# A selective scan with a routed feed-forward net on one core: GpSimd's products two states at a time, ranking inside its PSUM bank, new engine orders

## The chip, the cores and the metric

The kernel runs on one core of one Trainium2 chip. The metric is the device time of one execution in microseconds (us); smaller is better. Three runs of the kernel before took 1288.14, 1292.01 and 1292.46 us, a median of 1292.01. The engines are PE (TensorE), DVE (VectorE), ACT (ScalarE), POOL (GpSimd) and SP (SyncE, which here only issues transfers).

## The reference, cut to what matters

The input x is 16 sequences of 512 steps and 128 channels. Each goes through two layers with residual sums.

```python
# layer 1: selective scan, D_INNER = 256, D_STATE = 16
xn = layernorm(x)
x_proj, z = split(xn @ W_in + b_in)
u = silu(x_proj)
B, C = split(u @ W_xproj + b_xproj)
dt = softplus(u @ W_dt + b_dt)
#   per step t: h = h * exp(dt * A) + (dt * u) * B ;  y = sum over states of h * C + D * u
x = x + (y * silu(z)) @ W_out + b_out
# layer 2: shared expert and 8 routed experts, the best 2 weighed
xt = layernorm(x)
scores = softmax(xt @ gate_w.T)
chosen = top_k(scores + gate_bias, 2)
x = x + sum over e of mlp_e(xt) * weight_e + mlp_shared(xt)
#   mlp(x) = (silu(x @ w1.T) * (x @ w3.T)) @ w2.T, inner width 256
```

## The kernel before, in words

**Tiling.** Channels lie on the 128 partitions and the 512 steps of a sequence along the free axis. 256 inner channels are 2 halves, so one sequence has 2 x 16 = 32 scans, numbered 0 to 31 ("states" below), each over 128x512.

**One state's way.** ACT writes the decay exp(dt*A) into one of two PSUM banks (`da`, task `decay`, L589). POOL writes (dt*u)*B into one of four SBUF slots (`dbu`, L673). DVE scans the two (`scan`, L773). The product with C is then made either by DVE (`mul`, L781: the scan went to its PSUM bank, the product goes to a slot of `hc`) or by POOL (`hcp`, L681: the scan went to the `hc` slot, which is multiplied in place). `BY_DVE` says which: the 15 even states up to 28; POOL has the other 17. PE adds each product to `y_acc` by four transposing matmuls (`red`, L920). `hc` has four slots, so that scan or product of state a waits for the reduction of state a-4; `decay` of state a waits until state a-2 has left its bank.

**The second layer.** 9 experts x 2 halves = 18 units a sequence. PE makes `h1` and `h3` of a unit, each from three matmuls over 512 columns (L938), in three PSUM banks that take turns; ACT makes `silu` (L625), DVE `g` = silu * h3 (L815), PE `eo` (L907, 16 matmul records an expert), ACT scales by the router's weight (`sc`, L632) and DVE adds (`comb`, L823). Two more banks ("mixed") are shared in turn by all other matmuls: transposes of x and y (`x_t`, `gy`, `split`), `xp`, `z`, `bc`, `dl`, `proj`, `route`, `eo`.

**Router.** After `route`, ACT takes the exponential in the route bank and DVE does eight small steps (`rank.0` to `rank.7`, L697 to L717). Scores and biased scores lie in SBUF; the table of comparisons lies in the route bank. Step 4 (L708) subtracts the biased scores from themselves, 128x256 out of two SBUF operands. Step 7 (L717) writes `comb`, the weights.

**Normalisation.** DVE makes means and variances (L743, L751) and adds EPS (L754); POOL raises to the power -0.5 (L646, L649); DVE makes the shift (L761).

**Order.** Every engine follows a list written by hand or by a planner outside the kernel: `ORDER` is one pass of a loop ("window"), `START_ORDER` and `END_ORDER` are straight code before and after. `scan.5+1` is state 5 of the sequence after the window's own. Work of four sequences overlaps in a window. SP's queue loads x and the residual, and spreads B and C over all partitions in four groups a sequence (`spread`), each waiting until the states that read the old rows are done. Engines meet only at semaphores.

## Time and profile before

| what | us |
|---|---|
| median of three runs | 1292.01 |
| the profiled execution, whole | 1290.66 |
| its span, first to last instruction | 1288.5 |

The span and its rows come from the profiled execution; 2.2 us of that execution lie outside the span. A row of the engines gives busy time, not use: an engine that waits at a semaphore isn't busy. Rows that group instructions give the mean duration of one; neighbours on an engine overlap a little, so that the distance between two starts is shorter than the duration. "DMA" is the share of the core's transfer engines.

### The profile page before, as it was taken

Reading aid. Unit: us, or ns where it says so; the run is one execution under the profiler, and the core shown is the slowest. Engines: PE = TensorE matmul, PEld = TensorE weight load, DVE = VectorE, ACT = ScalarE, POOL = GpSimd, SP = SyncE. Lnnn points to the kernel's source line nnn. Section 1 sums busy time; section 2 is a strip of 40 time slices with the busy share of each in tenths; the row PEclk is TensorE's granted clock in tenths of the full one; section 3 lists DMA queues with packets and bytes.
Section 4 is the critical chain, followed back from the end, with each engine's and each line's share of the span. In section 5 each row is a group of like instructions: output and inputs, shape, how many; then the busy total and the mean of one; then the engine's idle time right before and its main releaser. Section 6 shows DMA issues by size and latency. Waiting matters only on the chain.

```text
span 1288.5 us, 25674 instructions
## 1 busy us (share of the span) xinstructions
PE 1179.8 (92%) x7200; PEld 946.2 (73%) x7200; DVE 1174.2 (91%) x1833; ACT 1126.6 (87%) x1965; POOL 1112.8 (86%) x902
## 2 busy tenths in 40 slices
PE   4565899999999999999999999999999999999998
PEld 2334587877878787787778777777878778788887
DVE  1779899999999999999999999999999999999954
ACT  6674889999998999999899999989989998999854
POOL 2999899898999989899998989999898999998700
PEclk8776899999999999999999999999999999999999
DMA  8233331605234160523415052331505243250000
GB/s 305 121 146 125 133 148 39 250 1 207 82 132 155 54 232 0 205 81 137 150 62 225 0 205 81 144 142 67 220 0 210 77 152 135 71 208 9 10 9 9
DMA packets 47942, 152.74 MB, mean 119 GB/s; under 512 B 4512, under 2 KB 29472, under 8 KB 31392
## 3 DMA queue, kind: packets, MB, share of 16 engines
q1 hardware_dynamic: 47904, 152.28, 31.3%
q8 instruction: 18, 0.29, 0.1%
q14 instruction: 20, 0.16, 0.0%
HBM read 147.03 MB, written 5.24 MB: 118 GB/s over the span
## 4 chain that ended last, share of the span: by engine, by line
POOL 27%; issue 23%; PE 22%; DVE 19%; ACT 7%; DVEq 1%; DMA 0%; POOLq 0%; ACTq 0%; SPq 0%
POOL dbu L673 16%; PE h L938 10%; POOL hc L681 7%; DVE da L773 6%; PE mixed L907 5%; DVE hc L773 5%; PE y_acc L920 4%; POOL dt_s L661 3%; DVE g L815 2%; ACT L625 2%; ACT silu L625 2%; ACT da L589 1%; DVE acc L823 1%; DVE stats L743 1%; DVE hc L781 1%
## 5 line engine op out<-in xcount | busy, mean ns | idle before, releaser
L673 POOL TENSOR_TENSOR dbu<-w_s,b_all 128x512 f32<-128x512 f32 x512 | 650.3, 1289 | 5.7 <-DVE da L773 3.0
L681 POOL TENSOR_TENSOR hc<-hc,c_all 128x512 f32<-128x512 f32 x272 | 350.5, 1292 | 82.1 <-DVE hc L773 80.6
L589 ACT ACTIVATE da<-dt_s,a_neg 128x512 f32<-128x512 f32 x512 | 346.7, 692 | 84.2 <-DVE hc L781 70.0
L773 DVE TENSOR_TENSOR_SCAN hc<-da,dbu 128x512 f32<-128x512 f32 x272 | 328.1, 1211 | 12.0 <-PE y_acc L920 10.9
L920 PE MATMUL y_acc<-ident,hc 128*128 128x128 f32 x2048 | 295.0, 280 | 32.5 <-POOL hc L681 27.3
L773 DVE TENSOR_TENSOR_SCAN da<-da,dbu 128x512 f32<-128x512 f32 x240 | 292.6, 1219 | 27.4 <-ACT da L589 15.1
L920 PEld LDWEIGHTS y_acc<-ident,hc 128*128 128x128 f32 x2048 | 247.5, 144 | 81.5 <-POOL hc L681 36.2
L907 PE MATMUL mixed<-w_s,g 128*128 128x128 f32 x2304 | 283.4, 276 | 3.2 <-DVE g L815 1.2
L907 PEld LDWEIGHTS mixed<-w_s,g 128*128 128x128 f32 x2304 | 270.6, 192 | 15.4 <-DVE g L815 10.1
L938 PE MATMUL h<-x_hi,w_hi 128*128 128x512 f32 x576 | 264.1, 458 | 7.4 <-DVE g L815 2.9
L938 PE MATMUL h<-x_hi,w_lo 128*128 128x512 f32 x576 | 228.4, 396 | 0.0
L938 PE MATMUL h<-x_lo,w_hi 128*128 128x512 f32 x576 | 227.9, 396 | 0.0
L815 DVE TENSOR_TENSOR g<-silu,h 128x512 f32<-128x512 f32 x288 | 193.4, 676 | 24.0 <-PE h L938 9.8
L625 ACT ACTIVATE silu<-h 128x512 f32<-128x512 f32 x288 | 158.6, 600 | 30.6 <-PE h L938 29.0
L781 DVE TENSOR_TENSOR hc<-da,c_all 128x512 f32<-128x512 f32 x240 | 163.9, 683 | 8.2 <-DVE da L773 2.6
L632 ACT ACTIVATE mixed<-mixed,comb 128x128 f32<-128x128 f32 x512 | 141.1, 337 | 20.4 <-PE mixed L907 20.3
L938 PEld LDWEIGHTS h<-x_hi,w_hi 128*128 128x128 f32 x576 | 109.3, 190 | 60.5 <-DVE g L815 32.5
L938 PEld LDWEIGHTS h<-x_hi,w_lo 128*128 128x128 f32 x576 | 108.4, 188 | 25.7
L589 ACT ACT_TABLE_LOAD x94 | 120.6, 1283 | 2.5 <-DVE hc L781 0.8
L938 PEld LDWEIGHTS h<-x_lo,w_hi 128*128 128x128 f32 x576 | 110.2, 191 | 12.1 <-issue 3.1
L625 ACT ACT_TABLE_LOAD x90 | 115.5, 1283 | 1.6
L823 DVE TENSOR_TENSOR acc<-mixed,acc 128x512 f32<-128x512 f32 x128 | 86.1, 673 | 8.7 <-ACT mixed L632 8.6
(77 smaller groups left out, 1063.6 us busy)
## 6 DMA issues: line engine op xcount, KB each, us to landing
b_all<-bc_rows SPq DMA_DIRECT2D x64, 1024.0 KB, 4.7
c_all<-bc_rows SPq DMA_DIRECT2D x64, 1024.0 KB, 6.8
xt<-in_x SPq DMA_DIRECT2D x16, 256.0 KB, 6.5
res<-in_x SPq DMA_DIRECT2D x16, 256.0 KB, 6.9
out<-acc SPq DMA_DIRECT2D x16, 256.0 KB, 2.3
silu<-in_w SPq DMA_DIRECT2D x6, 256.0 KB, 4.1
w_s<-in_w SPq DMA_DIRECT2D x1, 1152.0 KB, 6.9
bc_rows<-bc_rows_s SPq DMA_DIRECT2D x16, 64.0 KB, 1.6
```

Of the source, the lines that this page charges most:

```text
L589: act.activation(da[a % DA_SLOTS][:, :], dt_s[:, c, :], ACT.Exp, scale=a_neg[:, a:a + 1]).then_inc(decay_made, 1)
L625: act.activation(silu[:, a % SILU_SLOTS, :], h_tile("h1", a, n, off)[:, :], ACT.Silu).then_inc(silu_made, 1)
L632: last = act.activation(block_, block_, ACT.Copy, scale=comb[:, b, a - 1:a])
L673: pool.tensor_tensor(dbu[:, a % DBU_SLOTS, :], w_s[:, c, :], b_all[:, s, :], ALU.mult).then_inc(dbu_made, 1)
L681: pool.tensor_tensor(slot, slot, c_all[:, s, :], ALU.mult).then_inc(c_by_pool, 1)
L773: dve.tensor_tensor_scan(dst, ring[:, :], dbu[:, a % DBU_SLOTS, :], 0.0, ALU.mult, ALU.add).then_inc(scanned, 1)
L781: dve.tensor_tensor(hc[:, a % HC_SLOTS, :], da[a % DA_SLOTS][:, :], c_all[:, s, :], ALU.mult).then_inc(c_by_dve, 1)
L815: dve.tensor_tensor(g[:, a % G_SLOTS, :], silu[:, a % SILU_SLOTS, :], h_tile("h3", a, n, off)[:, :], ALU.mult).then_inc(g_made, 1)
L823: dve.tensor_tensor(acc[:, :, :], as_blocks(tile), acc[:, :, :], ALU.add).then_inc(freed, 1)
L907: last = pe.matmul(as_blocks(tile)[:, b, :], g[:, slot, b * P:(b + 1) * P], w2_s[:, at:at + DM], start=(f == 0), stop=(f == NF - 1))
L920: last = pe.matmul(y_acc[:, b, :], hc[:, a % HC_SLOTS, b * P:(b + 1) * P], ident[:, :], is_transpose=True, start=False, stop=(a % NS == NS ...
L938: last = pe.matmul(dst[:, :], w13_at(w, e, which, f), xx[:, :], start=(i == 0), stop=(i == len(parts) - 1))
```

## The change

1. **POOL works on pairs.** `dbu.k` now makes states 2k and 2k+1 in one instruction (128x1024, the operand dt*u repeated by a stride of zero), and `hcp.a` multiplies the slots of states a and a+1 by two rows of C. `dbu` has 8 slots in place of 4. The first scan of a pair waits for both products of `dbu`, and `hcp` waits for both scans.
2. **DVE has 16 states** in place of 15: 0, 1, 4, 5, ... 28, 29. POOL has 2, 3, 6, 7, ... 30, 31, eight pairs.
3. **Ranking reads its bank.** Scores and a second copy of the biased scores are kept in the route bank, so that no ranking step reads two SBUF operands. Step 3 becomes two instructions. The bank is now freed by step 7, not by step 6.
4. **EPS is added on POOL**, in `rs1` and `rs2` ahead of the power, with waits of its own.
5. **All orders are new.** The loop now runs over windows 4 to 13, and more of the program is straight code: START covers the first three sequences' scans.

Counted over one pass of the loop: ACT's table loads go from 13 to 14, POOL's instructions on 512 columns from 49 (32 + 17) to 24 on 1024 columns, DVE's products with C from 15 to 16. The other instructions of the loop are as many as before. In the whole program ACT's table loads go from 210 to 225.

```diff
-DA_SLOTS, DBU_SLOTS, HC_SLOTS = 2, 4, 4
+DA_SLOTS, DBU_SLOTS, HC_SLOTS = 2, 8, 4
+AT_ONCE = 2
+DBUS = STEPS // AT_ONCE
-BY_DVE = [0, 2, 4, 6, 8, 10, 12, 14, 16, 18, 20, 22, 24, 26, 28]
+BY_DVE = [0, 1, 4, 5, 8, 9, 12, 13, 16, 17, 20, 21, 24, 25, 28, 29]
 BY_POOL = [a for a in range(STEPS) if a not in BY_DVE]
+POOL_PAIRS = BY_POOL[::2]
...
 "pool":
-        hcp.7 dbu.10 dbu.11 rs1.0+1 dbu.12 dbu.13 hcp.9 hcp.11 dbu.14 dbu.15 hcp.13 dbu.16 rs2.0-1 dbu.17
+        dbu.15 rs1.0+2 hcp.26 dbu.0+1 hcp.30 dbu.1+1 dbu.2+1 dbu.3+1 hcp.2+1 resb.0 dbu.4+1 dbu.5+1 hcp.6+1
...
-                    act.wait_ge(route_steps, RANK_STEPS * (m + 1))
+                    act.wait_ge(*taken("route", 0, n, off))
...
                 elif what == "rs2":
+                    wait_apart(pool, moments2_made, m + 1)
+                    pool.tensor_scalar(var_eps2[:, :], moments2[:, :, 1], EPS, None, ALU.add).then_inc(var2_made, 1)
                     pool.wait_ge(var2_made, m + 1)
...
                 elif what == "dbu":
-                    c, s = a // NS, a % NS
+                    step = AT_ONCE * a
+                    c, s = step // NS, step % NS
...
-                    wait(pool, scanned, STEPS * m + a + 1 - DBU_SLOTS)
-                    pool.tensor_tensor(dbu[:, a % DBU_SLOTS, :], w_s[:, c, :], b_all[:, s, :],
-                                       ALU.mult).then_inc(dbu_made, 1)
+                    user, back = before(step + AT_ONCE - 1, DBU_SLOTS, STEPS)
+                    if not (isinstance(m, int) and m == 0 and back):
+                        pool.wait_ge(scanned, STEPS * (m - back) + user + 1)
+                    at = step % DBU_SLOTS
+                    pool.tensor_tensor(dbu[:, at:at + AT_ONCE, :], w_s[:, c, None, :].broadcast_to([P, AT_ONCE, T]),
+                                       b_all[:, s:s + AT_ONCE, :], ALU.mult).then_inc(dbu_made, 1)
                 elif what == "hcp":
                     s = a % NS
-                    pool.wait_ge(scanned, STEPS * m + a + 1)
+                    pool.wait_ge(scanned, STEPS * m + a + 2)
...
-                    slot = hc[:, a % HC_SLOTS, :]
-                    pool.tensor_tensor(slot, slot, c_all[:, s, :], ALU.mult).then_inc(c_by_pool, 1)
+                    at = a % HC_SLOTS
+                    pair = hc[:, at:at + 2, :]
+                    pool.tensor_tensor(pair, pair, c_all[:, s:s + 2, :], ALU.mult).then_inc(c_by_pool, 1)
...
                 elif i == 3:
-                    step = dve.tensor_tensor(biased[:, :, :], score[:, :, :],
-                                             gb_s[:, None, :].broadcast_to([P, NB, E]), ALU.add)
+                    for dst in (biased[:, :, :], other):
+                        step = dve.tensor_tensor(dst, score, gb_s[:, None, :].broadcast_to([P, NB, E]), ALU.add)
                 elif i == 4:
-                    step = dve.tensor_tensor(ahead, other, own, ALU.subtract)
+                    step = dve.tensor_tensor(ahead, other[:, :, None, :].broadcast_to([P, NB, E, E]), own, ALU.subtract)
...
                 elif i == 7:
-                    dve.wait_ge(*ranked)
                     wait(dve, scaled, E * m)
...
                 elif what in ("agg1", "agg2"):
-                    dve.wait_ge(done, m + 1)
-                    dve.tensor_scalar(var[:, :], mom[:, :, 1], EPS, None, ALU.add).then_inc(ready, 1)
...
                 elif what == "scan":
-                    dve.wait_ge(dbu_made, STEPS * m + a + 1)
+                    dve.wait_ge(dbu_made, DBUS * m + a // AT_ONCE + 1)
```

How the orders move work is seen at three places. On POOL, at the head of the loop, the kernel before has:

```order
L681 TENSOR_TENSOR hc<-hc,c_all 128x512
...
L673 TENSOR_TENSOR dbu<-w_s,b_all 128x512 x2
...
L646 TENSOR_TENSOR rstd<-var_eps,minus_half 128x4
...
L673 TENSOR_TENSOR dbu<-w_s,b_all 128x512
...
L681 TENSOR_TENSOR hc<-hc,c_all 128x512
```

and the changed one:

```order
L767 TENSOR_TENSOR dbu<-w_s,b_all 128x1024
...
L731 TENSOR_SCALAR var_eps<-moments 128x4
L733 TENSOR_TENSOR rstd<-var_eps,minus_half 128x4
...
L777 TENSOR_TENSOR hc<-hc,c_all 128x1024
...
L767 TENSOR_TENSOR dbu<-w_s,b_all 128x1024
...
L777 TENSOR_TENSOR hc<-hc,c_all 128x1024
```

The same products now come in instructions of twice the width, and the addition of EPS stands ahead of the power.

On DVE, the ranking steps 2 to 7 in the loop stand in the kernel before like this (`scan` is the SCALAR_TENSOR_TENSOR of L773, `mul` is L781):

```order
L703 TENSOR_TENSOR score<-mixed,inverse 128x32 [waits route_steps]
...
L705 TENSOR_TENSOR biased<-score,gb_s 128x32 [waits route_steps]
...
L708 TENSOR_TENSOR mixed<-biased 128x256 [waits route_steps]
...
L773 SCALAR_TENSOR_TENSOR da<-da,dbu 128x512 [waits dbu_made,decay_made]
...
L711 TENSOR_TENSOR mixed<-mixed,below 128x256 [waits route_steps]
...
L713 TENSOR_REDUCE rank<-mixed 128x32 [waits route_steps]
...
L717 SCALAR_TENSOR_TENSOR comb<-rank,score 128x32 [waits scaled]
```

and in the changed one (`scan` is L869, `mul` L877):

```order
L801 TENSOR_TENSOR mixed<-mixed,inverse 128x32 [waits route_steps]
...
L805 TENSOR_TENSOR biased<-mixed,gb_s 128x32 [waits route_steps]
L805 TENSOR_TENSOR mixed<-mixed,gb_s 128x32
...
L807 TENSOR_TENSOR mixed<-mixed,biased 128x256 [waits route_steps]
...
L869 SCALAR_TENSOR_TENSOR da<-da,dbu 128x512 [waits dbu_made,decay_made]
...
L810 TENSOR_TENSOR mixed<-mixed,below 128x256 [waits route_steps]
...
L812 TENSOR_REDUCE rank<-mixed 128x32 [waits route_steps]
...
L815 SCALAR_TENSOR_TENSOR comb<-rank,mixed 128x32 [waits scaled]
```

One operand of each step now lies in the bank ("mixed"), and one small instruction more is there.

On PE, in the loop, the transposes of y (`gy`) are the next user of the bank that `route` had. Before, `gy` follows ten tasks after `route`, the last of them (`eo`, a reduction, a unit's `h1`) being these:

```order
L907 MATMUL mixed<-w_s,g 128x128 [waits mixed_freed1,g_made]
L907 MATMUL mixed<-w_s,g 128x128 x7
...
L920 MATMUL y_acc<-ident,hc 128x128 [waits c_by_pool]
...
L938 MATMUL h<-x_hi,w_hi 128x512 [waits g_made]
...
L845 MATMUL mixed<-ident,y_s 128x128 [waits mixed_freed0]
```

In the changed order, from the same `eo` on (rows of like kind left out):

```order
L1003 MATMUL mixed<-w_s,g 128x128 [waits mixed_freed0]
...
L1034 MATMUL h<-x_hi,w_hi 128x512 [waits g_made]
...
L1016 MATMUL y_acc<-ident,hc 128x128 [waits c_by_pool]
...
L1034 MATMUL h<-x_hi,w_hi 128x512 [waits silu_made]
...
L1012 MATMUL y_acc<-ident,skip 128x128 [waits y_copied]
...
L941 MATMUL mixed<-ident,y_s 128x128 [waits mixed_freed1,y_copied]
```

Now 23 tasks stand between `route` and `gy`, eleven of them after that `eo`, so that the ranking has more of PE's work beside it.

## Rows read from the trace of the kernel before

**Rows 1.** The page: busy time, share of the span and instructions, by engine

```profile
PE 1179.8 (92%) x7200; PEld 946.2 (73%) x7200; DVE 1174.2 (91%) x1833; ACT 1126.6 (87%) x1965; POOL 1112.8 (86%) x902
```

**Rows 2.** Stretches: length, busy PE, PEld, DVE, ACT, POOL; clock, DMA share, GB/s

```profile
32.60:103.00 70.40, 38.03 (x162) 25.25 (x162) 56.83 (x57) 45.49 (x67) 69.72 (x55) 0.74 0.37 154
492.00:1090.50 598.50, 575.48 (x3584) 461.88 (x3584) 581.34 (x913) 557.31 (x977) 554.75 (x449) 1.00 0.33 124
1225.00:1288.50 63.50, 57.81 (x364) 50.47 (x361) 29.72 (x61) 31.12 (x77) 1.02 (x1) 0.99 0.03 9
```

**Rows 3.** DVE's timeline (start, length): the residual sum, once a window, eight windows apart

```profile
492.02 0.68 DVE L788 TENSOR_TENSOR res<-mixed,res 128x512 f32<-128x512 f32 x1
...
1090.57 0.68 DVE L788 TENSOR_TENSOR res<-mixed,res 128x512 f32<-128x512 f32 x1
```

**Rows 4.** Groups of instructions, 492.0 to 1090.5 us (count | busy, mean ns | idle before)

```profile
L673 POOL TENSOR_TENSOR dbu<-w_s,b_all 128x512 f32<-128x512 f32 x256 | 324.7, 1287 | 0.0
L681 POOL TENSOR_TENSOR hc<-hc,c_all 128x512 f32<-128x512 f32 x137 | 176.0, 1287 | 42.9 <-DVE hc L773 42.1
L589 ACT ACT_TABLE_LOAD x48 | 61.6, 1283 | 0.8
L881 PE MATMUL mixed<-xnT,win_s 128*128 128x512 f32 x64 | 31.5, 615 | 9.6 <-DVE acc L823 9.6
L661 POOL TENSOR_TENSOR dt_s<-soft,lin 128x512 f32<-128x512 f32 x16 | 22.0, 1378 | 0.0
L708 DVE TENSOR_TENSOR mixed<-biased 128x256 f32<-128x256 f32 x8 | 11.5, 1442 | 0.3
L845 PE MATMUL mixed<-ident,y_s 128*128 128x128 f32 x64 | 10.0, 279 | 8.4 <-DVE rank L713 8.4
L754 DVE TENSOR_SCALAR var_eps<-moments 128x4 f32<-128x4 f32 x16 | 9.9, 618 | 0.6
L649 POOL TENSOR_TENSOR rstd<-var_eps,minus_half 128x4 f32<-128x4 f32 x8 | 8.1, 1009 | 0.0
L717 DVE SCALAR_TENSOR_TENSOR comb<-rank,score 128x32 f32<-128x32 f32 x8 | 2.9, 364 | 0.0
L705 DVE TENSOR_TENSOR biased<-score,gb_s 128x32 f32<-128x32 f32 x8 | 2.4, 301 | 0.0
L703 DVE TENSOR_TENSOR score<-mixed,inverse 128x32 f32<-128x32 f32 x8 | 1.4, 180 | 0.0
```

**Rows 5.** Line 708 alone: shortest, median and longest of its instructions in ns

```profile
L708 DVE TENSOR_TENSOR mixed<-biased x16: 405/1440/1445, 163.3 to 1252.6; 128x256 f32<-128x256 f32 x16
```

**Rows 6.** POOL's timeline: a tiny fill, and products in a row

```profile
0.87 0.10 POOL L640 MEMSET minus_half<- 128x4 f32 x1
...
75.74 7.48 POOL L673 TENSOR_TENSOR dbu<-w_s,b_all 128x512 f32<-128x512 f32 x6
83.17 2.50 POOL L681 TENSOR_TENSOR hc<-hc,c_all 128x512 f32<-128x512 f32 x2
```

**Rows 7.** DVE's timeline: a scan, `g` and a product with C in a row

```profile
571.28 1.20 DVE L773 TENSOR_TENSOR_SCAN da<-da,dbu 128x512 f32<-128x512 f32 x1
572.40 0.67 DVE L815 TENSOR_TENSOR g<-silu,h 128x512 f32<-128x512 f32 x1
572.99 0.67 DVE L781 TENSOR_TENSOR hc<-da,c_all 128x512 f32<-128x512 f32 x1
```

**Rows 8.** The page's transfers: one group of C's rows, KB and us to landing

```profile
c_all<-bc_rows SPq DMA_DIRECT2D x64, 1024.0 KB, 6.8
```

**Rows 9.** Beginning, DVE's timeline: a two-operand split of weights

```profile
97.73 1.75 DVE L734 TENSOR_TENSOR w_lo<-silu,w_hi 128x512 fp32r<-128x512 f32 x1
```

**Rows 10.** The chain that ended last, near the end: seven units' matmuls, one `eo`

```profile
1249.53 4.92 PE h L938 x21
1254.44 1.78 PE mixed L907 x16
```

**Rows 11.** PE's timeline: one reduction

```profile
565.29 0.60 PE L920 MATMUL y_acc<-ident,hc 128*128 128x128 f32 x4
```

295 lines of the change are left out of this document (188 added, 107 removed).

## The prediction, made before the changed kernel ran

> **What bounds the kernel now.** I read the busy rows of the page first: PE 92%, DVE 91%, ACT 87%, POOL 86% [rows 1]. No engine stands out, so the stretches come next. In the middle the program is periodic: DVE's once-a-window sum starts at 492.02 and, eight windows later, at 1090.57 us [rows 3], which is 598.55 / 8 = 74.82 us a window. Divided by eight, the busy times of that stretch [rows 2] are DVE 72.7, PE 71.9, ACT 69.7 and POOL 69.3 us a window. The reader is to see two things. DVE is at 97%, and its load is the first floor; and all four are so close that taking work from one only uncovers the next. Each engine follows a fixed order, so what is left over (2.2 us above DVE's load) is the price of four orders that must mesh.
>
> The beginning is different. From 32.6 to 103.0 us POOL is busy 69.7 of 70.4 us, DVE 56.8 and ACT 45.5 [rows 2]: the second layer hasn't begun, and the products on POOL set the pace. At the end POOL is done, and PE works off the last units, busy 57.8 of 63.5 us [rows 2].
>
> The groups in the middle show the waits that bear on the change [rows 4]: POOL's `hcp` waited 42.1 us for scans, 5.3 a window; PE's `gy` waited 8.4 us (1.05 a window) for ranking, PE's matmuls of `xp` and `z` 9.6 us (1.2 a window) for DVE's `comb`.
>
> **The change, part by part, for one window.**
>
> DVE. One product with C more: `g`, on the same shapes, starts 0.59 us before the next instruction [rows 7], +0.6. The two additions of EPS go: 9.9 / 8 = -1.24 [rows 4]; each works on four columns and yet takes 618 ns in the mean. The subtraction of L708 takes 1442 ns in the middle, but 405 ns is the shortest [rows 4, 5]; the shortest one I take for the form that reads its bank, -1.03. L717 takes 364 ns and should fall to the 180 ns of L703, which has one operand in the bank: -0.18. L705 (301 ns) becomes two of 180 ns: +0.06. The sum is -1.8: DVE from 72.7 to 70.9 us.
>
> ACT. The new order needs 14 table loads in place of 13. One is 1283 ns [rows 4]: from 69.7 to 70.9 us. In the loop the cover of the extra load is 74.8 - 69.7 = 5.1 us of slack, of which it takes a quarter.
>
> POOL. 49 single instructions start 7.43 / 6 = 1.24 us apart [rows 6]: 60.7 us. They become 24 pairs. No row shows a pair. If POOL's time went wholly by columns, a pair would take 2 x 1.24 = 2.48 us. What is saved is the part of an instruction that doesn't depend on columns. The nearest rows for that are the fills, 0.10 us for 4 columns [rows 6], so I take 2.38 us. The far bound is the power on four columns, 1.01 us, as if all of it were fixed [rows 4]: 1.5 us. The other end is below nothing: `dt` has the same shape and costs 1378 ns against 1287 [rows 4], so a pair of a dearer form could take 2 x 1.33 = 2.66. Two additions of EPS come in, between a fill's 0.10 and the power's 1.01 us each; I take 0.3, nearer to the fill since there is no power in it. POOL: 69.3 - 60.7 + 24 x 2.38 + 0.6 = 66.3 us, with bounds of 45 (everything fixed) and 74.5 (2.66 a pair, 1.0 an addition).
>
> The Trainium skill ("GPSIMD Engine Reference", 3.1 Elementwise) gives 4497 ns for a two-operand instruction on 2048 columns, and a line through that and this trace's 1287 ns on 512 would make a pair 2.36 us long (an estimate); spaced as closely as the single ones it would be 2.31 us, and POOL at 64.7 in place of 66.3 us a window. No run here shows a pair yet.
>
> PE. The same matmuls, 71.9 us a window: PE is now the most loaded. Its waits are 74.8 - 71.9 = 2.9 us, and 2.25 of them are the two behind DVE. The one behind ranking should go: `gy` now stands 23 tasks after `route`, before ten, and the ranking loses over 1 us of its own. Step 7 holds the bank longer, but nobody asks for it that early. The one behind `comb` has no such reason. I let half of PE's waits go: a window of 71.9 + 1.45 = **73.4 us**. The other view, DVE's and ACT's new load of 70.9 plus the old 2.2 us of meshing, gives 73.1 and doesn't contradict it.
>
> SP. The spreads now wait for counts of pairs. The last group of a sequence is asked for seven pairs after it is released, 7 x 2.4 = 17 us, against 6.8 us for the transfer [rows 8]: I cost it at nothing. If that cover were gone, POOL would wait at `dbu.6`, and the scans behind it.
>
> **The whole program.** From the end of the second sequence's scans to the end of the last one's there are 14 windows: 14 x (73.4 - 74.8) = -19.9 us. Beginning: until the first `g`, the order of before has 58 `dbu` and 30 `hcp`, 88 x 1.24 = 109 us on the engine that sets the pace; the new one has 29 and 14 pairs, 43 x 2.38 = 102.3, plus 1 us of EPS: -5.7. Against it, the first scan starts one single later; I round to **-5.5**. Nine splits of weights on DVE read two SBUF operands, and one of them took 1.75 us [rows 9]. Each may now wait for a pair, up to 1.2 us longer, 11 us in all, on DVE, which has 70.4 - 56.8 = 13.6 us of slack in that stretch: I cost it at nothing.
>
> The rule behind it stands in the Trainium skill ("SBUF — State Buffer", Who interferes with whom): a DVE instruction with two SBUF operands and a GpSimd instruction that reads SBUF exclude each other for a whole instruction. By that rule longer POOL instructions make each such meeting dearer; the trace agrees (405 against 1440 ns for one line), and in the loop the change leaves no instruction of that kind.
>
> End: after the last reduction the new order leaves 46 of `h1`/`h3` and 13 `eo`, before 45 and 12. One is 4.92 / 7 = 0.70, an `eo` 1.78 us [rows 10]: **+2.5 us**.
>
> Sum: 1288.5 - 19.9 - 5.5 + 2.5 = 1265.6 us of span; with the 2.2 us around it **1268 us**. The profiled execution (1290.7) is 1.3 us below the median of the three (1292.0), which is within what they scatter. I forecast 1268, 1.9% below the median.
>
> **The rivals.**
>
> *The window falls further.* PE's true load is below its busy rows, which include overlaps: at the end an `h` takes only 0.70 us [rows 10]. Then DVE and ACT at 70.9 are the floor, and POOL's slack of 8 us lets the orders mesh at 1.2 us above it: 72.1 us, 14 x -2.7 = -38, in all 1250. For it: 5.3 us of POOL's waits for scans a window show how tight POOL's part was. Against it: three engines are still at 97%.
>
> *Nothing is gained in the loop.* PE's waits are replaced, for instance by scans that wait for pairs; the window stays at 74.8. Then only beginning and end count: 1290.7 - 5.5 + 2.5 = 1288 us, the same.
>
> *The pair's latency decides (slower).* A scan of POOL's into an `hc` slot must wait for the reduction of the same slot four states ago: the second scan of a pair, 2.4 us of product (1.24 before), up to one `dbu` pair in front of it (2.4), and a reduction, 0.6 us [rows 11], with hand-overs about 0.9: 5.7 us. Meanwhile DVE has two scans of 1.12 [rows 7], two products of 0.59, and other work: 70.9 us for eight groups of four states, less 4 x 1.12 and 2 x 0.59 in each, leaves 3.2 us a group. That is 6.6 us. If PE comes to the reduction over 0.9 us late, the pair becomes the wait. With 1.5 us in two of the eight groups a window is 76.4: 14 x +1.6 = +22, and 1288.5 + 22 - 5.5 + 2.5 + 2.2 is 1310. For it: an `eo` of 1.78 us ahead of the reduction is enough. Against it: POOL has more slack than before.
>
> *Pairs cost more than two.* At 2.66 us POOL has 74.5 us a window and is the bound, with 1 us of meshing 75.5: 14 x 0.7 = +10, and at the beginning 43 x 2.66 = 114 against 109 us, with EPS +6: 1290.7 + 10 + 6 + 2.5 = 1309 us. That is the case in which the change doesn't do what it says. Only the price of `dt` speaks for it, and `hcp`, in place in one tile, costs no more than `dbu` [rows 4].
>
> **How the numbers follow.** Forecast 0.64, with its own range 1256 to 1280; window falls further 0.12; nothing gained 0.12; latency 0.08; dear pairs 0.04. What a measurement can tell from no change is 0.5%, 6.5 us, that is 1285.5 to 1298.5. The first two are faster, and a quarter of the third: 0.79. The rest of the third is the same: 0.09. The last two are slower: 0.12. The range takes in the second and third case and leaves out the last two: 1249 to 1296.
>
> **What would show it.** Right: rows of `dbu` on 1024 columns near 2.4 us; L807 near 0.41 us; windows of 73.4 us, with PE at 98%; POOL's wait for scans above 5.3 us a window; the first `h` some 5 us earlier than before. Wrong: `hc` scans of POOL's states that wait for `y_acc` by over 1 us a window; ACT busy below 95% of a window, since decays wait for DVE; PE waiting behind `comb` as much as before or more.

## The result, and the profile after

The changed kernel takes 1247.57 us (median; 1247.2 to 1250.07 in four runs), beside 1291.03 us for the kernel before in the same session. The ratio is 0.967, with a 95% interval of 0.9648 to 0.9692: 43 us less. The forecast was 1268 with a range of 1249 to 1296, so the sign was right and the size was not: the gain is nearly twice the one forecast, and the time lies just under the range. The profiled execution took 1250.07 us, its span is 1248.3.

The busy line of the page after, which answers to [rows 1] (PE is 94% busy now, and POOL down to 84%):

```profile
PE 1167.9 (94%) x7200; PEld 952.1 (76%) x7200; DVE 1140.5 (91%) x1833; ACT 1140.1 (91%) x1980; POOL 1043.5 (84%) x534
```

The stretches after, with the columns of [rows 2]. The first answers to the beginning, the second is seven windows of the loop, the third is the very end:

```profile
32.60:103.00 70.40, 37.01 (x152) 26.86 (x152) 61.54 (x72) 46.87 (x70) 64.54 (x30) 0.62 0.38 149
541.30:1041.80 500.50, 497.15 (x3134) 406.17 (x3133) 488.40 (x799) 493.31 (x861) 453.64 (x232) 1.00 0.33 128
1185.00:1248.30 63.30, 57.78 (x370) 51.09 (x368) 30.84 (x64) 30.07 (x78) 1.27 (x2) 1.00 0.03 9
```

DVE's timeline (start, length): the residual sum, seven windows apart, as in [rows 3]:

```profile
541.36 0.68 DVE L884 TENSOR_TENSOR res<-mixed,res 128x512 f32<-128x512 f32 x1
...
1041.80 0.68 DVE L884 TENSOR_TENSOR res<-mixed,res 128x512 f32<-128x512 f32 x1
```

A window is 500.44 / 7 = 71.49 us, before 74.82. (The last of the seven, 70.98 us, already runs out of the loop; the windows that lie wholly in it take 71.57.) Divided by seven, the busy times of the second stretch are PE 71.0, ACT 70.5, DVE 69.8, POOL 64.8. PE is busy for 99.3% of the time, and its waits behind DVE's `comb` and behind ranking, 2.25 us a window in [rows 4], are gone. The groups of that stretch:

```profile
L767 POOL TENSOR_TENSOR dbu<-w_s,b_all 128x1024 f32<-128x1024 f32 x113 | 266.9, 2386 | 1.3 <-DMA c_all<-bc_rows 1.3
L777 POOL TENSOR_TENSOR hc<-hc,c_all 128x1024 f32<-128x1024 f32 x56 | 133.4, 2383 | 43.2 <-DVE hc L869 43.2
L977 PE MATMUL mixed<-xnT,win_s 128*128 128x512 f32 x56 | 29.1, 600 | 0.0
L941 PE MATMUL mixed<-ident,y_s 128*128 128x128 f32 x56 | 8.4, 272 | 0.0
L807 DVE TENSOR_TENSOR mixed<-mixed,biased 128x256 f32<-128x256 f32 x7 | 2.9, 419 | 0.0
L805 DVE TENSOR_TENSOR biased<-mixed,gb_s 128x32 f32<-128x32 f32 x7 | 1.2, 177 | 0.0
```

The whole span falls into three parts, cut at the fourth residual sum and ten windows later: length, then busy times as above. The kernel before, and then the changed one:

```profile
0.00:342.40 342.40, 271.13 (x1511) 208.06 (x1511) 287.65 (x429) 274.24 (x447) 301.74 (x248) 0.89 0.38 146
342.40:1090.60 748.20, 719.32 (x4480) 577.36 (x4480) 726.72 (x1142) 696.71 (x1221) 693.46 (x561) 1.00 0.33 124
1090.60:1288.50 197.90, 189.37 (x1209) 160.81 (x1209) 159.84 (x266) 155.63 (x299) 117.56 (x95) 1.00 0.14 51
```

```profile
0.00:326.60 326.60, 257.02 (x1436) 199.91 (x1437) 277.90 (x428) 270.15 (x435) 279.94 (x148) 0.86 0.41 153
326.60:1041.80 715.20, 710.60 (x4478) 580.52 (x4477) 697.95 (x1141) 705.08 (x1230) 648.81 (x331) 1.00 0.33 128
1041.80:1248.30 206.50, 200.26 (x1292) 171.66 (x1290) 164.63 (x267) 164.90 (x317) 114.74 (x57) 1.00 0.14 54
```

The parts change by -15.8, -33.0 and +8.6 us, -40.2 in all. The last one is longer since more is left to do there: 1292 matmul records in place of 1209. The first is shorter for the same reason, 1436 in place of 1511, and because it begins faster. The ten windows in the middle hold the same matmuls (4478 and 4480) and are the gain proper.

### The profile page after: what moved, and what is told of

It is laid out like the page before. It is cut to its first block, busy times and chain, and to the rows that moved or that the text cites. A ratio compares the mean times of both kernels' runs of the same rounds, so it can differ in the third digit from the quotient of the medians.

```text
span 1248.3 us, 24503 instructions
## 1 busy us (share of the span) xinstructions
PE 1167.9 (94%) x7200; PEld 952.1 (76%) x7200; DVE 1140.5 (91%) x1833; ACT 1140.1 (91%) x1980; POOL 1043.5 (84%) x534
## 4 chain that ended last, share of the span: by engine, by line
POOL 44%; PE 23%; issue 18%; ACT 9%; DVE 3%; DMA 1%; POOLq 1%; ACTq 0%; DVEq 0%; SPq 0%
POOL dbu L767 31%; PE h L1034 10%; POOL hc L777 8%; PE mixed L1003 6%; PE y_acc L1016 4%; ACT da L674 2%; POOL w_s L754 2%; POOL dt_s L750 2%; DVE hc L869 1%; ACT mixed L717 1%; ACT silu L710 1%; PE mixed L984 1%; DMA c_all<-bc_rows 1%; ACT L674 1%; PE mixed L977 1%
## 5 line engine op out<-in xcount | busy, mean ns | idle before, releaser
L767 POOL TENSOR_TENSOR dbu<-w_s,b_all 128x1024 f32<-128x1024 f32 x256 | 606.5, 2392 | 1.5 <-DMA c_all<-bc_rows 1.3
L777 POOL TENSOR_TENSOR hc<-hc,c_all 128x1024 f32<-128x1024 f32 x128 | 305.4, 2386 | 109.1 <-DVE hc L869 106.6
L674 ACT ACTIVATE da<-dt_s,a_neg 128x512 f32<-128x512 f32 x512 | 341.9, 687 | 43.2 <-DVE hc L869 24.1
L869 DVE TENSOR_TENSOR_SCAN hc<-da,dbu 128x512 f32<-128x512 f32 x256 | 302.0, 1212 | 26.3 <-ACT da L674 18.6
L869 DVE TENSOR_TENSOR_SCAN da<-da,dbu 128x512 f32<-128x512 f32 x256 | 308.4, 1216 | 14.0 <-POOL dbu L767 12.4
L1016 PEld LDWEIGHTS y_acc<-ident,hc 128*128 128x128 f32 x2048 | 251.8, 146 | 76.5 <-POOL hc L777 35.8
L1034 PE MATMUL h<-x_hi,w_hi 128*128 128x512 f32 x576 | 273.0, 474 | 9.3 <-ACT silu L710 6.3
L710 ACT ACTIVATE silu<-h 128x512 f32<-128x512 f32 x288 | 161.3, 600 | 19.0 <-PE h L1034 15.7
L877 DVE TENSOR_TENSOR hc<-da,c_all 128x512 f32<-128x512 f32 x256 | 171.8, 678 | 4.9 <-PE y_acc L1016 3.8
```

The lines of the kernel that those rows point to most:

```text
L674: act.activation(da[a % DA_SLOTS][:, :], dt_s[:, c, :], ACT.Exp, scale=a_neg[:, a:a + 1]).then_inc(decay_made, 1)
L710: act.activation(silu[:, a % SILU_SLOTS, :], h_tile("h1", a, n, off)[:, :], ACT.Silu).then_inc(silu_made, 1)
L767: pool.tensor_tensor(dbu[:, at:at + AT_ONCE, :], w_s[:, c, None, :].broadcast_to([P, AT_ONCE, T]), b_all[:, s:s + AT_ONCE, :], ALU.mult).t ...
L777: pool.tensor_tensor(pair, pair, c_all[:, s:s + 2, :], ALU.mult).then_inc(c_by_pool, 1)
L869: dve.tensor_tensor_scan(dst, ring[:, :], dbu[:, a % DBU_SLOTS, :], 0.0, ALU.mult, ALU.add).then_inc(scanned, 1)
L877: dve.tensor_tensor(hc[:, a % HC_SLOTS, :], da[a % DA_SLOTS][:, :], c_all[:, s, :], ALU.mult).then_inc(c_by_dve, 1)
```

## The experiments

Every run is compared with the kernel before on the same chip, whose medians were 1290.2 to 1292.4 us. The changed kernel itself was timed only beside the first result, so that differences from its 1247.57 us are differences between sessions. "Window" is the distance of residual sums in the loop. Three questions led: which part of the change brings the loop's 3.3 us a window; why some variants of the changed kernel are so much slower; and which engine is the bound, before and after.

### Undoing one part each

EPS back on DVE:

```diff
-                    wait_apart(pool, moments1_made, m + 1)
-                    pool.tensor_scalar(var_eps[:, :], moments[:, :, 1], EPS, None, ALU.add).then_inc(var1_made, 1)
...
+                    dve.wait_ge(done, m + 1)
+                    dve.tensor_scalar(var[:, :], mom[:, :, 1], EPS, None, ALU.add).then_inc(ready, 1)
```

> The changed kernel with one part undone: EPS is added on DVE again, not on POOL. Theory 'load' (a window is the load of the busiest engine plus a little meshing): DVE has two instructions more a window, 0.62 us each in the kernel before and up to twice that beside the longer POOL instructions; DVE goes from 69.8 to 71.0 to 72.0 us a window and the window from 71.5 to 72 to 73, in all 1255 to 1268 us. Rival 'orders' (the new orders carry the gain, the small edits nothing): 1247 to 1251 us. Rival 'pairs' (POOL's pairs carry it): 1247 to 1251 us too.

Measured: 1299.36 us, ratio 1.0068 (1.0043 to 1.0093), windows of 75.8 to 77.1. Against the changed kernel that is a loss of 52 us for two instructions on four columns. The whole gain and more was gone, which none of the expectations had.

Ranking with scores and biased scores in SBUF again:

```diff
+        score_s = sb("score", [P, NB, E])
...
-                    for dst in (biased[:, :, :], other):
-                        step = dve.tensor_tensor(dst, score, gb_s[:, None, :].broadcast_to([P, NB, E]), ALU.add)
+                    step = dve.tensor_tensor(other, score, gb_s[:, None, :].broadcast_to([P, NB, E]), ALU.add)
```

> The changed kernel with one part undone: ranking keeps its scores and biased scores in SBUF again, so that its steps read two SBUF operands (the bank is still freed by step 7). Theory 'load': the subtraction goes from about 0.4 to 1.4 us or, if it waits for a whole POOL pair, to 2.8; DVE 69.8 to 71.0 to 72.5 us a window, in all 1255 to 1275 us. Rivals 'orders' and 'pairs': 1247 to 1251 us.

Measured: 1299.65 us, ratio 1.0082 (1.0055 to 1.0109), a window of 75.12. The groups of this run from 500 to 1000 us:

```profile
L803 DVE TENSOR_TENSOR biased<-score,gb_s 128x32 f32<-128x32 f32 x7 | 16.7, 2392 | 0.0
L805 DVE TENSOR_TENSOR mixed<-biased 128x256 f32<-128x256 f32 x6 | 13.0, 2166 | 0.0
```

Both instructions read two operands in SBUF, and each takes about as long as a whole pair on GpSimd (2386 ns). With one operand in the bank they take 177 and 419 ns, and a second copy of 0.19 us is needed. That is 3.8 us more on DVE, and the window grows by 3.6. The time lies above everything expected. The body of DVE's loop has 292 instructions here and no gap, so that the cause of the next section has no part in it.

Single products in the new orders:

```diff
-                    pool.tensor_tensor(dbu[:, at:at + AT_ONCE, :], w_s[:, c, None, :].broadcast_to([P, AT_ONCE, T]),
-                                       b_all[:, s:s + AT_ONCE, :], ALU.mult).then_inc(dbu_made, 1)
+                    for k in range(AT_ONCE):
+                        last = pool.tensor_tensor(dbu[:, at + k, :], w_s[:, c, :], b_all[:, s + k, :], ALU.mult)
+                    last.then_inc(dbu_made, 1)
```

and the same for `hcp`.

> The changed kernel with one part undone: each of POOL's pairs is made by two instructions of 512 columns, at the same places in the order and with the same semaphores. Starts are 2.34 us apart for a pair and 1.24 for a single one, so POOL gets 24 x 0.14 = 3.4 us a window more, 65.1 to 68.5, under a window of 71.5. Theory 'load': that fits into POOL's slack, 1248 to 1256 us. Rival 'pairs' (the cheaper products set the pace): the window grows by most of the 3.4 us, 1275 to 1295 us. Rival 'orders': 1247 to 1252 us.

Measured: 1258.15 us, ratio 0.975 (0.973 to 0.9771), a window of 72.41. The pairs are worth 10.6 us; three quarters of the gain are there without them. GpSimd's load still fits, as the first theory had it, but its latency shows: from 500 to 1000 us, PE waits once in every window for a product with C, 0.8 us, and this wait is absent with pairs.

```profile
PE y_acc L1018 <- POOL hc L778: 5.6, 7, 0.8
```

All three undone, so that only the new orders (and the sixteenth state of DVE) are left:

> The changed kernel with EPS on DVE, ranking in SBUF and POOL's products by single instructions, all three together: what is left of the change is the new orders, eight slots of dbu and 16 states on DVE. Theory 'load': DVE 72.3 us and more, a window of 73 to 74, 1268 to 1282 us; the rest of the gain, 10 to 20 us, is the orders'. Rival 'orders': under 1256 us. Rival 'the work alone': 1285 us and more.

Measured: 1309.42 us, ratio 1.0158 (1.0128 to 1.0188), windows of 76.1 to 77.8. I read this at first as "the new orders are bad by themselves". Later runs show that most of it had another cause.

### A second cause: the length of DVE's loop

In the first run above, DVE's timeline shows a gap of 2.6 to 3.2 us at the instruction that begins the loop's body, at each of the loop's nine jumps back. "issue" means that the engine waited for nothing that the profile shows. Seven of the nine gaps are marked so. The other two are put down to PE, whose matmul happened to end less than 1 us before:

```profile
462.63 0.69 DVE L909 TENSOR_TENSOR g<-silu,h 128x512 f32<-128x512 f32 x1 [2.68 <-PE h L1032]
...
615.04 0.69 DVE L909 TENSOR_TENSOR g<-silu,h 128x512 f32<-128x512 f32 x1 [3.12 <-issue]
```

The page counts the packets that bring instructions: 71 on queue q14, against 26 for the changed kernel. 40 of the 71 lie between the first and the last jump back, where the changed kernel has none. The variant had made the body longer. So I made only the body longer:

```diff
+                    if a in (2, 3, 4, 5):
+                        dve.sem_inc(passed, 1)
                     if a == 0:
                         wait(dve, stored, 16 * m)
```

> The changed kernel with four more semaphore increments a window on DVE, which compute nothing: only the body of DVE's loop is longer. Theory of the length (the 3.1 us gaps at the loop's back edge, seen where the EPS additions stood on DVE again, come from a body that is too long to be kept): gaps of about 3 us marked 'issue' at most back edges, instruction packets of DVE's queue near 70 in place of 26, a window of about 74, 1270 to 1285 us. Rival (the gaps belong to the EPS additions themselves): no gap, 26 packets, a window within 0.3 us of 71.57, 1247 to 1252 us.

Measured: 1281.65 us, ratio 0.9919 (0.9898 to 0.994). Four instructions a window that compute nothing cost 34 us. All nine jumps back have a gap, of 3.2 to 3.9 us, windows are 74.9 to 75.9, and the packets are these (count, MB, share):

```profile
q14 instruction: 71, 0.58, 0.2%
```

The control puts the same four increments into the kernel before, and then twenty:

```diff
+                    if a in (2, 3, 4, 5):
+                        for _ in range(5):
+                            dve.sem_inc(passed, 1)
```

> The kernel before with the four semaphore increments a window on DVE that cost the changed kernel 34 us. The body of DVE's loop has 12 visible instructions fewer here. Theory (the length of the body decides): no gaps, 20 packets of instructions, 1288 to 1294 us. Rival (the increments cost the time by themselves, by upsetting the engine's waiting): 1310 to 1330 us.

Measured: 1290.17 us, ratio 0.9992 (0.998 to 1.0004), 20 packets, no gap. The increments by themselves cost nothing. (The "12 visible instructions fewer" of the expectation is wrong: both bodies have 114 instructions that count as busy, and they differ in waits and increments.)

> The kernel before with twenty more semaphore increments a window on DVE in place of four, which makes the body of its loop longer than that of the changed kernel with four. Theory (the length of the body decides, whatever the orders): gaps of about 3 us at the back edge, packets of instructions over 60, 1305 to 1335 us. Rival (the refetch belongs to the new orders): no gaps, 20 to 22 packets, under 1297 us.

Measured: 1311.08 us, ratio 1.0148 (1.0129 to 1.0167), 76 packets on q14, gaps of 2.0 to 2.2 us at all eleven jumps back (eight marked "issue"), windows of 76.1 to 77.6. So a longer body costs this in either set of orders. Counted with waits and increments, the body of DVE's loop is 288 instructions before, 293 after, 292 in the control with four, 297 and 308 in the two that lost, 295 in the first run and 294 in the fourth. The fourth run has 72 packets and gaps of 2.8 to 3.4 us at all nine jumps; only three of them are marked "issue":

```profile
468.28 0.69 DVE L909 TENSOR_TENSOR g<-silu,h 128x512 f32<-128x512 f32 x1 [3.04 <-PE h L1032]
...
620.79 0.69 DVE L909 TENSOR_TENSOR g<-silu,h 128x512 f32<-128x512 f32 x1 [3.16 <-issue]
```

Of the kernels in new orders, all with up to 293 are free and all with 294 and more are hit: the changed kernel stands at the edge.

How much of the first run's 52 us was waiting for GpSimd, then? My first try to shorten the body made two-column instructions of the shifts:

```diff
-                    for b in range(NB):
-                        last = dve.tensor_scalar(sh[:, b:b + 1], mom[:, b, 0:1], r[:, b:b + 1], -1.0,
+                    for b in range(0, NB, 2):
+                        last = dve.tensor_scalar(sh[:, b:b + 2], mom[:, b:b + 2, 0], r[:, b:b + 1], -1.0,
```

> The additions of EPS on DVE again, as in the first run, but the shift of each norm is made by two instructions in place of four (each on two blocks with one block's factor, which leaves the others' values wrong): the body of DVE's loop is four instructions shorter and DVE's load 0.5 us less. Theory that the additions' waits behind GpSimd's pairs are the larger part: no gaps at the back edge, 26 packets, yet a window of 74 to 75.5, 1275 to 1290 us. Rival that the refetch at the back edge is nearly all: a window below 72.5, 1248 to 1262 us.

Measured: 1353.3 us, ratio 1.0473 (1.0456 to 1.0491), windows of 79.6 to 80.8, the slowest of all, with no gap and 27 packets. Neither expected time held. The line's own rows say why (shortest, median and longest in ns; first the shifts of the changed kernel on one column, then those of this run on two, then the additions of EPS on four columns in the first run):

```profile
L857 DVE TENSOR_SCALAR shift<-moments,rstd x128: 179/202/214, 6.6 to 1192.4; 128x1 f32<-128x1 f32 x128
```

```profile
L855 DVE TENSOR_SCALAR shift<-moments,rstd x64: 197/2174/2437, 6.3 to 1296.0; 128x2 f32<-128x2 f32 x64
```

```profile
L848 DVE TENSOR_SCALAR var_eps<-moments x32: 169/432/2386, 4.9 to 1238.3; 128x4 f32<-128x4 f32 x32
```

A one-tensor instruction of DVE on one column never waits for GpSimd in 128 cases; on two or four columns it can last as long as a whole pair. That makes a prediction of its own, which was put to the kernel before:

```diff
-                    dve.tensor_scalar(var[:, :], mom[:, :, 1], EPS, None, ALU.add).then_inc(ready, 1)
+                    for b in range(NB):
+                        last = dve.tensor_scalar(var[:, b:b + 1], mom[:, b, 1:2], EPS, None, ALU.add)
+                    last.then_inc(ready, 1)
```

> The kernel before, with each addition of EPS on DVE made as four instructions on one column each, as the shifts are made (204 ns each, of which none was seen to wait for GpSimd, while two-column ones took 1495 ns in the mean). Theory (an instruction of DVE on one column doesn't wait for GpSimd's instruction, one on two or four does): the rows show about 200 ns each and none above 400, DVE's load falls by 1.24 - 2 x 4 x 0.14 = about 0.1 us a window but loses its long waits, a window of 74.2 to 74.8, 1281 to 1291 us. Rival (every such instruction may wait, and the shifts only fall where GpSimd is idle): means above 600 ns, rows up to 1440 ns, a window above 75.5, over 1300 us.

Measured: 1280.44 us, ratio 0.9913 (0.9896 to 0.9929), a window of 74.13: 12 us gained with three more instructions at each place, none of which waits. That is slightly more than the theory expected.

```profile
L755 DVE TENSOR_SCALAR var_eps<-moments x128: 141/144/156, 5.0 to 1221.2; 128x1 f32<-128x1 f32 x128
```

The Trainium skill ("VectorE: DVE Perf Modes", Mode 2×_2P) lets a one-tensor instruction with its operands in SBUF use both of DVE's read ports where its outermost dimension longer than one is even, or odd and equal in both tensors; two and four columns are even, and one column has no such dimension. The trace agrees in who waits (2174 ns in the median on two columns, at most 214 on one); which ports an instruction used it doesn't show.

Now the clean split. EPS is on DVE again, and of each norm's four one-column shifts only two are made:

```diff
-                    for b in range(NB):
+                    for b in range(2):
                         last = dve.tensor_scalar(sh[:, b:b + 1], mom[:, b, 0:1], r[:, b:b + 1], -1.0,
```

> The changed kernel with EPS added on DVE again (four columns at once, as in the first run), and of each norm's four one-column shifts only two made (blocks 2 and 3 take those of 0 and 1, so their values are wrong): the body of DVE's loop is four instructions shorter than in the first run. The first run lost 52 us, the longer body alone cost 34. Theory that the two causes add up: no gaps at the back edge, 26 packets of instructions, 1247.6 + 18 = 1260 to 1272 us. Rival (the waits for GpSimd alone account for the 52 us): 1290 to 1302 us.

Measured: 1267.2 us, ratio 0.9826 (0.9808 to 0.9843), a window of 73.08, 26 packets, no gap. EPS on DVE costs 20 us without the longer body, the longer body alone 34 (above), together 54; the first run had lost 52. The two causes add up, within what the missing shifts hide: four instructions of 0.20 us a window are left out here, so that 20 is rather too low.

> The new orders alone (EPS on DVE, ranking in SBUF, single products), with two shifts of four left out as in the run above, so that the body of DVE's loop is short enough. The same without the shortening gave 1309 us with three gaps of 3.3 us in the loop. Theory (the new orders are bad as long as DVE waits for GpSimd in the ranking): 1294 to 1304 us, a window near 75.5. Rival (they lost only by the long body): 1275 to 1290 us.

Measured: 1283.39 us, ratio 0.9934 (0.991 to 0.9957). Five executions fell into two groups, 1276 and 1283.5, and why stays open; the profiled one is of the first and has windows of 73.43. The fourth run's loss was therefore the long body: it is 26 us slower than the slower group here, and its nine gaps add up to 27. My reading of it was wrong. Whether the new orders gain anything by themselves isn't shown clearly: of the 7 us or more against the kernel before, the four shifts that are left out of each window can explain a large part.

### DVE relieved in the old orders

```diff
                 if what == "rs1":
+                    wait_apart(pool, moments1_made, m + 1)
+                    pool.tensor_scalar(var_eps[:, :], moments[:, :, 1], EPS, None, ALU.add).then_inc(var1_made, 1)
...
-                    step = dve.tensor_tensor(biased[:, :, :], score[:, :, :],
-                                             gb_s[:, None, :].broadcast_to([P, NB, E]), ALU.add)
+                    for dst in (biased[:, :, :], other):
+                        step = dve.tensor_tensor(dst, score[:, :, :], gb_s[:, None, :].broadcast_to([P, NB, E]), ALU.add)
```

> The kernel before, with its orders and single products, with EPS added on GpSimd and the ranking reading the bank for the subtraction only. DVE's load falls by 1.24 + 1.03 = 2.3 us a window. Theory (DVE's instructions that wait for GpSimd upset both sets of orders, the orders themselves hardly matter): a window of 72.5 to 73.5, 1260 to 1275 us. Rival (the gain needs the new orders, since the old ones are meshed around those waits): a window of 74.3 to 74.8, 1283 to 1292 us.

Measured: 1279.87 us, ratio 0.9903 (0.9886 to 0.992), a window of 73.93. This lies between the two expectations. The groups from 492 to 1090 us show that the subtraction had only handed its wait on, to the copy ahead of it:

```profile
L711 DVE TENSOR_TENSOR mixed<-score,gb_s 128x32 f32<-128x32 f32 x8 | 10.5, 1318 | 0.0
```

That copy reads two operands in SBUF. With the score in the bank too, it doesn't:

```diff
-                    step = dve.tensor_tensor(score[:, :, :], expd, each_block(inverse, E), ALU.mult)
+                    for dst in (score[:, :, :], banked):
+                        step = dve.tensor_tensor(dst, expd, each_block(inverse, E), ALU.mult)
```

> The kernel before, with its orders and single products, with EPS added on GpSimd, and the ranking with its score in the bank as well (written twice, so that the last step reads the one in SBUF and the bank is given back as early as before). In the earlier run with old orders only the subtraction had been moved to the bank, and the wait of 1.3 us went to the copy ahead of it, which read two operands in SBUF. Here neither reads two. DVE's load falls by another 1.1 us a window. Theory (old orders take up DVE's relief at less than half): a window of 73.3 to 73.7, 1270 to 1276 us, against 1258 us for the new orders with single products. Rival (the orders are worth nothing, the relief is all): 1256 to 1262 us, a window near 72.5. Third possibility: the wait moves on to the last step, which still reads two operands in SBUF, and the time stays at 1280.

Measured: 1272.22 us, ratio 0.9855 (0.9838 to 0.9873), a window of 73.36. The copy is down to 189 ns, and part of the wait has moved on once more, to the last step, which still reads two (364 ns in [rows 4]):

```profile
L713 DVE TENSOR_TENSOR mixed<-mixed,gb_s 128x32 f32<-128x32 f32 x8 | 1.5, 189 | 0.0
L724 DVE SCALAR_TENSOR_TENSOR comb<-rank,score 128x32 f32<-128x32 f32 x8 | 7.7, 964 | 0.0
```

Set beside each other, the runs in old orders show that the window follows DVE's busy time nearly one for one (seven windows of each, divided by seven; light PE comes further below):

| old orders | window | DVE busy | window less DVE | PE busy |
|---|---|---|---|---|
| before | 74.82 | 72.67 | 2.15 | 71.9 |
| EPS by columns | 74.13 | 72.05 | 2.08 | 71.8 |
| EPS on GpSimd, subtraction in the bank | 73.93 | 71.80 | 2.13 | 71.7 |
| all relief | 73.36 | 71.24 | 2.12 | 72.0 |
| light PE | 74.08 | 72.27 | 1.82 | 65.3 |

The row of "all relief" is this stretch (columns as in [rows 2]):

```profile
488.34:1001.85 513.51, 504.14 (x3136) 404.33 (x3136) 498.68 (x799) 485.69 (x855) 486.60 (x407) 1.00 0.34 126
```

This gives the decomposition. DVE's relief in the old orders: 1290.2 to 1272.2, 18 us. The new orders, with the sixteenth state, the eight slots and what was left of the ranking's wait: to 1258.2, 14 us. The pairs: to 1247.6, 10.6 us. This sequence of the steps is mine, and the parts don't stand alone: with pairs but with the ranking in SBUF (second run) a kernel takes 1299.65 us, with single products and no relief at all 1276 to 1284 (the run above with two shifts).

### Which engine is the bound

PE made lighter by a third of the experts' first matmuls, in both kernels:

```diff
-                    parts = ((w13_hi, x2_hi), (w13_hi, x2_lo), (w13_lo, x2_hi))
+                    parts = ((w13_hi, x2_hi), (w13_hi, x2_lo))
```

> The kernel before with the third product of each h1 and h3 left out (a third of PE's work on the experts, outputs less exact). Theory (before, DVE with its waits for GpSimd set the window and PE had slack): a window of 74.3 to 74.8, and only the end shortens, by over 10 us. Rival (PE with 71.9 and its waits set the window, as the prediction had it): a window below 73.5.

> The changed kernel with the third product of each h1 and h3 left out (the low part of the weights), which takes about a third of PE's work on the experts away and leaves the outputs less exact. If PE is the bound of a window (busy 71.0 of 71.57 us), the window falls to DVE's and ACT's load with their meshing, 70.5 to 71.0 us in the loop, and the end after the last reduction, all PE, shortens by over 10 us. If the engines' rows hide slack on PE, the window stays at 71.4 to 71.6 and only the end shortens.

Measured (one execution each, as are the light ACT and the light DVE below): before, 1275.66 us and a window of 74.08; after, 1234.05 us and a window of 71.12. From 500 to 1000 us, the kernel before and then the changed one, both with light PE (columns as in [rows 2]):

```profile
500.00:1000.00 500.00, 440.44 (x2779) 342.07 (x2777) 487.71 (x767) 468.67 (x828) 466.24 (x379) 1.00 0.34 129
```

```profile
500.00:1000.00 500.00, 459.24 (x2892) 354.17 (x2890) 490.66 (x800) 494.18 (x868) 456.40 (x233) 1.00 0.33 129
```

Before, PE has 6.6 us a window less to do and the window gives up 0.74: PE was not the bound. After, it has 5.7 less and the window gives up 0.4, since ACT and DVE are next: ACT is busy 494 of 500 us.

ACT and DVE made lighter in the changed kernel:

```diff
-                    for b in range(NB):
-                        block_ = as_blocks(tile)[:, b, :]
-                        last = act.activation(block_, block_, ACT.Copy, scale=comb[:, b, a - 1:a])
-                    last.then_inc(scaled, 1)
+                    act.activation(tile[:, :], tile[:, :], ACT.Copy, scale=comb[:, 0, a - 1:a]).then_inc(scaled, 1)
```

> The changed kernel with each scaling of an expert's output done by one instruction for all four blocks in place of four (three blocks' outputs take the wrong factor): ACT's load falls by 8 x (1.35 - 0.6) = 6 us a window. If ACT with 70.5 is what bounds the window (leaving out a third of PE's products gave only 71.12), it falls to PE's 71.0 at most and perhaps less, 70.0 to 71.1, and then PE is next. If PE or DVE bounds it, it stays at 71.4 to 71.6.

```diff
-                        dve.tensor_tensor(acc[:, :, :], as_blocks(tile), acc[:, :, :], ALU.add).then_inc(freed, 1)
+                        dve.tensor_tensor(acc[:, 0:2, :], as_blocks(tile)[:, 0:2, :], acc[:, 0:2, :], ALU.add).then_inc(freed, 1)
```

> The changed kernel with each later sum of the experts' outputs done on half of the columns (half of the outputs lack those experts): DVE's load falls by 8 x 0.25 = 2 us a window, from 69.8. DVE isn't the most loaded, so the theory that the window is bound by PE and ACT expects 71.3 to 71.6 us. If DVE's order is what the others wait for (GpSimd's and ACT's waits for its scans), 70.5 to 71.1.

Measured: light ACT 1242.31 us and a window of 71.00, light DVE 1244.73 us and 71.38. (The light DVE has a gap of 3.7 us behind the loop, at 1179 us, so that the windows are the better measure.) With ACT out of the way PE is busy 499.1 of 500 us:

```profile
500.00:1000.00 500.00, 499.10 (x3157) 408.24 (x3156) 490.31 (x808) 476.28 (x697) 458.37 (x233) 1.00 0.33 129
```

So 70.9 us is what PE needs in a window; ACT's 70.5 and DVE's 69.8 are just behind, and meshing costs 0.6 us. Making any single engine lighter brings at most 0.6 us a window.

An attempt at a better version moved ACT's product of u and D to GpSimd, from the fourth sequence on:

```diff
+                    if a == 0 and not (isinstance(m, int) and m <= 2):
+                        pool.wait_ge(*taken("xp", 1, n, off))
+                        pool.wait_ge(reduced, STEPS * (m - 1) + NS + 1)
+                        for c in range(NC):
+                            pool.tensor_tensor(skip[:, c, :], u[:, c, :], d_s[:, c:c + 1].broadcast_to([P, T]),
+                                               ALU.mult).then_inc(skip_made, 1)
```

> The changed kernel with the product of u and D (two ACT instructions of 0.71 us a window) made by GpSimd behind the first product of dt and u, from the fourth sequence on: ACT's load falls by 1.4 us to 69.1 a window, GpSimd's rises by 2.6 to 67.5. Theory (PE at 70.9 is the floor, ACT at 70.5 adds half a microsecond of meshing to it): a window of 71.2 to 71.5, 1242 to 1247 us. Rival (GpSimd's 2.6 us come between dbu and the scans that wait for it): a window of 71.8 to 73, 1251 to 1266 us.

Measured: 1268.06 us, ratio 0.9827 (0.9813 to 0.9841), a window of 73.26. It is slower, a little beyond the rival's range: GpSimd has 6.7 us a window to spare, and 2.1 us in one place (two of 1050 ns) cost 1.7 us of every window. The waits from 500 to 1000 us name another path than the rival's. No scan waits for `dbu`; GpSimd's products with C come late, PE waits 1.7 us a window for them, and ACT and DVE behind:

```profile
ACT da L676 <- DVE hc L877: 16.6, 21, 1.7
PEld y_acc L1024 <- POOL hc L785: 16.5, 13, 2.1
...
PE y_acc L1024 <- POOL hc L785: 11.8, 7, 1.7
...
DVE hc L877 <- PE y_acc L1024: 6.9, 7, 1.0
```

No run that computes all of the reference to the same precision beat the changed kernel.

## Why the prediction was right or wrong, point by point

**Sizes of the single terms: right.** A pair takes 2386 ns (forecast 2.38), so "pairs cost more than two" is out. The subtraction takes 419 ns (0.41), `comb`'s last step 178 (0.18), an addition of EPS on POOL 0.24 (0.3). POOL's busy time is 64.8 us a window, forecast 66.3. Counted as number times mean duration, DVE's rows fall from 80.2 to 78.3 us a window, -1.9 (forecast -1.8), and ACT's rise from 77.3 to 78.2, +0.9 (+1.2).

**The window: wrong, and the failed step is PE's.** The prediction said "71.9 us a window: PE is now the most loaded" and added half of its waits, 1.45 us: 73.4 in all. Measured are 71.5, of which PE is busy 71.0 and waits 0.5.

Half of the miss is the waits. The one behind ranking and most of the one behind `comb` go with DVE's relief alone, in the old orders (from 500 to 1000 us, 2.3 us are left of 8.0 behind `comb`), so that "the one behind `comb` has no such reason" was wrong: it was a wait behind DVE's lateness.

The other half is the load. With the same number of matmuls PE is busy for 71.0 us after, although its rows, as number times mean, add up to slightly more (145.4 against 144.8 us). Rows overlap, and busy time is their union; DVE's union, too, fell by 2.9 us where its rows fell by 1.9. So 71.9 was no floor. That fewer interruptions let the rows overlap more would be one reason, but the runs don't bear it out: with all relief in the old orders most of PE's waits are gone and it is still busy for 72.0 us. In the new orders, over seven windows each, it is 71.8 us without relief, 71.3 with it and 71.1 with pairs. So the fall needs the new orders, and its cause stays open.

What the prediction left out can be named by its own terms. It gave the new orders nothing but the wait behind ranking, and the pairs nothing in the loop, since POOL had slack. The relief alone, in the old orders and without the sixteenth state and the extra table load, makes a window of 73.36; that this is the 73.4 forecast is chance, since the sum gave the relief no such part. From there the new orders bring 0.95 us (72.41) and the pairs 0.84 (71.57), the latter with PE's wait of 0.8 us for GpSimd's product. The light PE in the kernel before shows that PE was hardly a bound there, and the table above points to DVE.

**Meshing: wrong.** The cross-check took DVE's and ACT's 70.9 plus the old 2.2 us. For the old orders such a sum holds (the table above: 2.1 us over DVE in four kernels), and it is a better account of them than PE's load. DVE's waits behind GpSimd are no part of that price, since it stays at 2.1 us with most of them gone. Nor are they random: in the eight windows of the kernel before the subtraction always takes the same time, and of the two additions of EPS one always takes 1.03 to 1.06 us and the other 0.18 to 0.20.

```profile
L708 DVE TENSOR_TENSOR mixed<-biased x8: 1435/1443/1445, 536.4 to 1060.2; 128x256 f32<-128x256 f32 x8
```

It is the new orders and the pairs that mesh closer: 1.7 us over DVE now, and 0.6 over PE.

**The beginning: right.** Forecast -5.5 us. The first matmul of an expert, PE's timeline before and after:

```profile
147.58 0.47 PE L938 MATMUL h<-x_hi,w_hi 128*128 128x512 f32 x1
```

```profile
141.73 0.48 PE L1034 MATMUL h<-x_hi,w_hi 128*128 128x512 f32 x1 [0.39 <-DVE x_lo L891]
```

That is 5.9 us earlier. The splits of weights did wait for pairs, as feared: the six of one form now take 1.98 us each, before 1.19. That is 4.7 us in all, within DVE's slack, and the beginning came out as forecast.

**The end: right as a term, but the last window was not foreseen.** PE's timeline, the first matmul behind the last reduction, before and after:

```profile
1225.19 0.48 PE L938 MATMUL h<-x_hi,w_hi 128*128 128x512 f32 x1
```

```profile
1183.04 0.48 PE L1034 MATMUL h<-x_hi,w_hi 128*128 128x512 f32 x1
```

From there to the end of the span it is 63.3 us before and 65.3 after, 2 us more where 2.5 were forecast, with 46 of `h1`/`h3` and 13 `eo` as counted. The 8.6 us by which the last of the three parts above grew begin earlier. The scans of one sequence end 71.1 to 72.2 us after those of the one before, except for the last, which takes 81.7 us (before 78.0): work had been put off into that window. So 13 of the 14 windows brought 3.2 us each and the last one cost 3.7, in all -37.8 where -19.9 was forecast. By the prediction's own parts the whole is -5.8 (forecast -5.5), -37.8 (-19.9) and, behind the last scan, +3.4 (+2.5): -40.2 us. The window was missed by 1.9 us, which makes 27 us in 14 windows; the last window took some 9 of them back, and that was luck. These are the last scans of the second and of the last sequence on DVE's timeline (start, length), before and then after:

```profile
170.06 2.33 DVE L773 TENSOR_TENSOR_SCAN hc<-da,dbu 128x512 f32<-128x512 f32 x2
...
1220.66 2.33 DVE L773 TENSOR_TENSOR_SCAN hc<-da,dbu 128x512 f32<-128x512 f32 x2
```

```profile
165.40 1.21 DVE L869 TENSOR_TENSOR_SCAN hc<-da,dbu 128x512 f32<-128x512 f32 x1
...
1177.05 2.34 DVE L869 TENSOR_TENSOR_SCAN hc<-da,dbu 128x512 f32<-128x512 f32 x2
```

**SP: right.** The spreads cost 1.3 us of waiting in seven windows.

**The rivals.** "The window falls further" (72.1 us a window, 1250 us) was nearest to what came. Two things that it names are shown: PE's load is below the 71.9 of its busy rows, and POOL's shorter products let the others mesh (0.84 us a window, the run with single products). Its floor was not DVE and ACT at 70.9, though, but PE at 70.9 (light ACT), and its -38 us for 14 windows met the measured -37.8 partly by luck, since 13 windows gained 3.2 us each where it had 2.7, and the last one lost. It got 0.12, because I gave weight to "three engines are still at 97%"; they are at 98 to 99% now. "The pair's latency decides" had a real seed: POOL's waits for scans are 6.2 us a window (5.3 before), and POOL's slack covers them. The run with the product on GpSimd shows how near it is: 2.1 us more in one place, and it decides.

The rule on DVE and GpSimd that the prediction weighed for the beginning mattered in the loop: relieving DVE is 18 of the 43 us. To price the lost waits as durations (1.24 + 1.03 us) was sound for that part, since in the old orders the window fell by as much as DVE's busy time. It says nothing of the other 25 us.
